# Another order of the attention sum, GpSimd's work and the odd batches' products in a kernel with pairwise Strassen K and V

## The reference

```python
def _L0_xattn_ref(x, context, context_mask, Wq, bq, Wkv, bkv, Wo, bo):
    q = x @ Wq + bq
    kv = context @ Wkv + bkv
    k, v = jnp.split(kv, 2, axis=-1)
    ...
    q = _larope(q, Lq)
    k = _larope(k, Lk)
    scores = jnp.einsum('bhqd,bhkd->bhqk', q, k) * SCALE
    scores = jnp.where(context_mask[:, None, None, :], scores, -jnp.inf)
    attn = jax.nn.softmax(scores, axis=-1)
    out = jnp.einsum('bhqk,bhkd->bhqd', attn, v)
    out = out.transpose(0, 2, 1, 3).reshape(B, Lq, H * hd)
    return out @ Wo + bo
...
x = x + _L0_xattn_ref(_layernorm(x, axis=-1), ctx_1024, mask_BxS2_bf1, ...)
x = x + _L0_attn_ref(_layernorm(x, axis=-1), ...)
x = x + _L0_ffn_ref(_layernorm(x, axis=-1), ...)
```

## Time and profile before

| what | value |
|---|---|
| median of 3 runs | 830.67 us (829.15 to 832.28) |
| profiled execution, its own time | 831.04 us |
| its span, first to last instruction | 829.2 us |
| cross attention, end of the last batch's step | about 585 us |
| TensorE busy | 760.4 us, 92% |
| VectorE busy | 574.8 us, 69% |
| ScalarE busy | 408.2 us, 49% |
| GpSimd busy | 340.0 us, 41% |
| mean granted TensorE clock | 0.961 |

### The profile page before, as it was taken

How to read it: one execution, slowest core, us unless ns; L and a number is a source line. 1 busy time by engine, 2 the same in 40 slices (tenths; PEclk the granted TensorE clock), 3 DMA queues, 4 the chain that set the end, 5 groups by cost and what they waited for, 6 DMA issues and landing times. The chain is left out here.

```text
span 829.2 us, 23209 instructions
## 1 busy us (share of the span) xinstructions
PE 760.4 (92%) x9494; PEld 660.5 (80%) x9495; DVE 574.8 (69%) x1293; ACT 408.2 (49%) x930; POOL 340.0 (41%) x364
## 2 busy tenths in 40 slices
PE   8999979979997997999899799798889999789997
PEld 7998869878896986888798688787667777668884
DVE  6766876975876686597577668746679998932236
ACT  5435646553563554555455464535447666213330
POOL 1654445454443644436354354522123222036740
PEclk9999999998999998999899999999999999969999
DMA  8211201111011010110101011013483234834548
GB/s 289 112 53 40 73 5 49 60 64 53 16 47 52 9 53 1 54 59 2 53 8 54 19 35 60 2 52 120 145 349 154 115 140 174 319 123 165 189 140 304
DMA packets 23317, 78.99 MB, mean 95 GB/s; under 512 B 3344, under 2 KB 4752, under 8 KB 20144
## 3 DMA queue, kind: packets, MB, share of 16 engines
q1 hardware_dynamic: 19536, 65.50, 21.7%
q0 software_dynamic: 3680, 12.06, 4.3%
HBM read 58.93 MB, written 18.61 MB: 94 GB/s over the span
## 5 line engine op out<-in xcount | busy, mean ns | idle before, releaser
L167 PE MATMUL quad<-wparts,othi 128*128 128x512 f32 (+1 forms) x104 | 49.2, 473 | 33.1 <-DVE otlo L1019 33.1
L501 POOL TENSOR_TENSOR wraw<-craw 128x516 f32<-128x516 f32 x14 | 18.6, 1326 | 135.9 <-issue 131.0
L1356 PE MATMUL bank<-ctx_parts_hi,wparts 128*128 128x258 f32 x224 | 68.7, 307 | 0.8 <-DVE ctx_parts_lo L890 0.7
L890 DVE TENSOR_TENSOR ctx_parts_lo<-craw,ctx_parts_hi 128x1032 fp32r<-128x1032 f32 (+1 forms) x56 | 64.8, 1158 | 2.6 <-ACT ctx_parts_hi L626 2.6
L1381 PE MATMUL bank<-wparts,ctx_parts_hi 128*128 128x256 f32 x224 | 64.6, 288 | 0.3 <-DVE kb_even L962 0.3
L1357 PE MATMUL bank<-ctx_parts_hi,wparts 128*128 128x258 f32 x224 | 63.5, 283 | 0.0
L1358 PE MATMUL bank<-ctx_parts_lo,wparts 128*128 128x258 f32 x224 | 63.4, 283 | 0.0
L1383 PE MATMUL bank<-wparts,ctx_parts_hi 128*128 128x256 f32 x224 | 63.0, 281 | 0.0
L1384 PE MATMUL bank<-wparts,ctx_parts_lo 128*128 128x256 f32 x224 | 62.8, 280 | 0.0
L626 ACT ACTIVATE ctx_parts_hi<-craw 128x1032 fp32r<-128x1032 f32 (+1 forms) x56 | 47.2, 843 | 26.9 <-POOL craw L509 26.6
L661 ACT ACTIVATE wraw<-wraw,nmax 128x257 f32<-128x257 f32 x96 | 47.9, 501 | 23.9 <-DVE nmax L983 23.9
(11 more groups left out here) (413 smaller groups left out, 2719.4 us busy)
## 6 DMA issues: line engine op xcount, KB each, us to landing
craw<-ctx_t_dram SPq DMA_DIRECT2D x32, 516.0 KB, 4.3
expert_lo<-weights_dram SPq DMA_DIRECT2D x8, 1024.0 KB, 12.2
expert_hi_scratch<-wraw SPq DMA_DIRECT2D x16, 512.0 KB, 2.6
wparts<-expert_hi_scratch SPq DMA_DIRECT2D x8, 1024.0 KB, 8.6
wraw<-weights_dram SPq DMA_DIRECT2D x6, 1024.0 KB, 4.9
expert_lo<-ffn_out_scratch SPq DMA_DIRECT2D x16, 256.0 KB, 5.2
x<-x_dram SPq DMA_DIRECT2D x8, 256.0 KB, 4.5
craw<-weights_dram SPq DMA_DIRECT2D x2, 1024.0 KB, 4.9
```

Source lines behind the costliest of these rows:

```text
L167: pe.matmul(psum, ahi(c), bhi(c), start=(c == 0), stop=False)
L890: dve.tensor_tensor(dst[1], src, dst[0].bitcast(F32), ALU.subtract).then_inc(s_clo, 1)
L1356: pe.matmul(psum, whi_i[:, i, cols], hi[:, i, :], start=own and i == 0, stop=False, skip_group_check=not own)
```

## The change

No instruction is added, removed or altered in size; only the order on four engines changes, from batch 3 to batch 30.

- **VectorE:** `o_sum(b-1)` comes first in every step, in front of `masked`; in even steps `v_sum(p, S_11)` too. `o_lo(b-1)` comes right behind `masked` in even steps (before: behind `k_cos` and the layer norm's statistics), and right behind `pair_parts` in odd steps.
- **GpSimd:** `o_bias(b-1)` comes first in every step. In odd steps `diagonals` and the first `k_sin` come ahead of `ctx_sums_early`. In even steps `ctx_sums_late` comes ahead of `diagonals`.
- **ScalarE:** `o_hi(b-1)` comes ahead of the exponentials in even steps, and ahead of `k_copy(p, 0, 4)` in odd ones. `k_copy(q, 0, 1)` comes ahead of `part_hi(q, O_T4)`. `v_copy(p, 5)` moves from the even step's start to the odd step's end.
- **TensorE, odd steps:** K product (0, 4) ahead of the transposes, (1, 1) ahead of (1, 3), (1, 6) ahead of the extra step, `diagonals_spread` and `attend` in the middle of the step, V product 2 behind 5 and behind K product (1, 4). Even steps keep their order.

```diff
--- before.py
+++ after.py
@@ -306,10 +306,10 @@
             L_HI, L_LO, L_PRODUCT, L_COPY, L_SUM = range(1, 6)
 
 
-            K_PRODUCTS = ((0, 2), (0, 5), (0, 1), (0, 6), (0, 3), (0, 7), (1, 2), (1, 5), (0, 4), (1, 3), (1, 1), (1, 6),
+            K_PRODUCTS = ((0, 2), (0, 5), (0, 1), (0, 6), (0, 3), (0, 7), (1, 2), (1, 5), (0, 4), (1, 1), (1, 3), (1, 6),
                           (1, 7), (1, 4))
             K_COPIES = ((0, 5), (0, 1), (0, 6), (1, 5), (0, 4), (1, 1), (1, 6), (1, 4))
-            V_PRODUCTS = (2, 5, 1, 6, 3, 7, 4)
+            V_PRODUCTS = (5, 2, 1, 6, 3, 7, 4)
             V_COPIES = (5, 1, 6, 4)
 
             def k_product_of(q, c, k):
@@ -570,24 +570,24 @@
                         if b == PLAIN - 2:
                             ctx_sums_late(q)
                     elif b % 2 == 1:
+                        o_bias(b - 1)
+                        diagonals(b)
+                        if b < B - 1:
+                            k_sin(b + 1, 0)
                         if q <= PAIR_LAST:
                             ctx_sums_early(q)
-                        o_bias(b - 1)
-                        if b < B - 1:
-                            k_sin(b + 1, 0)
-                        diagonals(b)
                         if b < B - 1:
                             k_sin(b + 1, 1)
                         ln_and_bias(t, j)
                         if b < B - 1:
                             k_sin(b + 1, 2)
                     else:
+                        o_bias(b - 1)
                         for i in range(3):
                             k_sin(b + 1, i)
-                        o_bias(b - 1)
-                        diagonals(b)
                         if q <= PAIR_LAST:
                             ctx_sums_late(q)
+                        diagonals(b)
                         ln_and_bias(t, j)
                 ln_pool(pool, TILES + 1)
                 o_bias(B - 1)
@@ -790,10 +790,10 @@
                     p, q = b // 2, b // 2 + 1
                     more = q <= PAIR_LAST
                     last = t == TILES - 1
-                    v_copy(p, 5)
                     v_copy(p, 1)
                     if more:
                         part_hi(q, O_X1)
+                    before_o_hi(b)
                     exp(b, 0)
                     exp(b, 1)
                     v_copy(p, 6)
@@ -805,12 +805,11 @@
                     for g in range(G):
                         pt_evac(b, g)
                     v_copy(p, 4)
-                    before_o_hi(b)
                     if more:
                         part_hi(q, O_T32)
                         k_copy(q, 0, 5)
+                        k_copy(q, 0, 1)
                         part_hi(q, O_T4)
-                        k_copy(q, 0, 1)
                     if j == 0:
                         ln_apply(t + 1, x[:, 0 if last else t + 1, :])
                     if more:
@@ -824,23 +823,24 @@
                     for g in range(G):
                         exp(b, g)
                     k_copy(p, 1, 5)
+                    before_o_hi(b)
+                    k_copy(p, 0, 4)
                     pt_evac(b, 0)
                     pt_evac(b, 1)
-                    k_copy(p, 0, 4)
+                    k_copy(p, 1, 1)
                     pt_evac(b, 2)
                     pt_evac(b, 3)
-                    k_copy(p, 1, 1)
-                    next_mask(b)
-                    before_o_hi(b)
+                    k_copy(p, 1, 6)
                     if j == 1:
                         xt_hi(t + 1)
-                    k_copy(p, 1, 6)
                     if j == 3:
                         qt_evac(t + 1)
+                    next_mask(b)
                     if q <= PAIR_LAST:
                         part_hi(q, O_T1)
+                    v_copy(p, 5)
                     k_copy(p, 1, 4)
-                    if b == PLAIN - 1:
+                    if b == PAIR_FIRST * 2 - 1:
                         w_hi(WO)
                     if last:
                         act.wait_ge(s_qmm, TILES)
@@ -1136,13 +1136,14 @@
                     p, q = b // 2, b // 2 + 1
                     more = q <= PAIR_LAST
                     last = t == TILES - 1
+                    o_sum(b - 1)
+                    v_sum(p, S_11)
                     begin_step(b, j)
-                    v_sum(p, S_11)
+                    o_lo(b - 1, (b - 1) % BT)
                     if more:
                         part_lo(q, O_X1)
                     v_sum(p, S_12)
                     v_sum(p, S_22)
-                    o_sum(b - 1)
                     inverse_sums(b)
                     pair_parts(b)
                     if more:
@@ -1153,7 +1154,6 @@
                         if t == 2:
                             dve.wait_ge(s_x, 16 * (TILES - 1))
                         ln_stats(t + 1, x[:, 0 if last else t + 1, :])
-                    o_lo(b - 1, (b - 1) % BT)
                     if more:
                         part_lo(q, O_T32)
                     if j == 0:
@@ -1171,21 +1171,21 @@
                 def odd_step(b, t, j):
                     p, q = (b + 1) // 2, (b + 3) // 2
                     last = t == TILES - 1
+                    o_sum(b - 1)
                     begin_step(b, j)
                     k_sum(p, 0, S_12)
                     k_sum(p, 0, S_22)
                     if j == 3:
                         q_rotate(t + 1)
-                    o_sum(b - 1)
                     inverse_sums(b)
                     pair_parts(b)
+                    o_lo(b - 1, (b - 1) % BT)
                     k_cos(b + 1, 0)
                     k_sum(p, 1, S_11)
                     k_cos(b + 1, 1)
-                    o_lo(b - 1, (b - 1) % BT)
+                    k_sum(p, 1, S_12)
                     if j == 1:
                         xt_lo(t + 1)
-                    k_sum(p, 1, S_12)
                     k_sum(p, 1, S_22)
                     if q <= PAIR_LAST:
                         part_lo(q, O_T1)
@@ -1561,18 +1561,18 @@
                     k_product(p, 0, 7)
                     k_product(p, 1, 2)
                     k_product(p, 1, 5)
+                    k_product(p, 0, 4)
                     probs_transposed(b)
-                    k_product(p, 0, 4)
+                    k_product(p, 1, 1)
                     k_product(p, 1, 3)
-                    k_product(p, 1, 1)
+                    k_product(p, 1, 6)
                     extra_step(b, t, j)
-                    k_product(p, 1, 6)
-                    v_product(p, 2)
+                    diagonals_spread(b)
+                    attend(b, j)
                     k_product(p, 1, 7)
                     v_product(p, 5)
                     k_product(p, 1, 4)
-                    diagonals_spread(b)
-                    attend(b, j)
+                    v_product(p, 2)
                     v_product(p, 1)
 
                 def last_step(b, j):
```

## The result

| | before | after |
|---|---|---|
| median | 830.71 us (829.15 to 832.28, 4 runs) | 777.09 us (776.16 to 778.46, 4 runs) |
| profiled execution | 831.04 us | 776.16 us |
| mean granted TensorE clock | 0.961 | 0.986 |

The ratio of the times is 0.9356, with a 95% interval from 0.9331 to 0.9381: 6.4% faster, 53.6 us. The prediction said 43.7 us. The time lies 0.1 us inside its range (777 to 804) and outside the 781 to 794 that it took for likeliest.

A forecast was written before the change was run, and what follows sets the result against it. The prediction took TensorE's own work to bound the kernel, held up by waits for `o_lo`. It put 55.8 us removed against 12.1 added, 43.7 net, giving 787.0 us, 5.3% faster, likeliest 781 to 794, range 777 to 804.

The forecast's parts named there:

- The bound and the main wait: TensorE's work sets the end; seven output products wait for VectorE's `o_lo`, late only by its place: 33.1 us saved.
- The slow clock, 13.9: TensorE's seven output products run at a clock that fell during the wait before them; full clock saves 13.9 us.
- K product (0, 6), 3.9: Last K product of even steps waits 0.64 us for `k_copy(q, 0, 1)` behind a `part_hi`; turning them round saves 3.9.
- Odd steps, 4.9 saved and 1.4 added: `o_bias` first frees `o_hi` and K copies, 4.9 us saved; K products sharing one bank, delayed by copies, add 1.4.
- undisturbed ones take 16.04: Odd steps that nothing delays take 16.04 us; the 13 together exceed 13 times that by 4.9 us.
- Diagonals with j = 2, 6.0: GpSimd's second diagonal, behind VectorE's `part_lo(O_T32)`, ends at 14.0, 1.0 us after TensorE comes; six steps add 6.0.
- O_T32 with j = 0, 1.4: `part_lo(O_T32)` ends about when K product (0, 6) needs it; 0.2 us latency in seven steps adds 1.4, below 0.
- Batches 4 and 30, 3.3: `o_sum` and a `v_sum` ahead of VectorE's masks delay V product 7 by about 1.65 us; both batches add 3.3.
- The first: Rival: diagonals, O_T32 and copies come just in time, only batches 4 and 30 cost; 778.5 us, chance 0.12.
- VectorE did not become the bound: Rival: VectorE becomes the bound, masks come 1.5 us late in 13 odd steps, 16 us more; 803 us, chance 0.15.
- The third: Rival: slower, as TensorE waits at `diagonals_spread` in all 13 even steps and the clock falls; 846 us at w = 3, chance 0.04.
- The fourth: Rival: `o_hi` sits behind `part_hi(O_X1)` on ScalarE, so the stall only moves; about 827 us, chance 0.04.

The follow-up runs named there:

- experiment 1: Changed kernel with `o_lo` of the even steps back behind `k_cos` and the statistics on VectorE; 804.16 us, ratio 0.9706 to the kernel before.
- experiment 4: Kernel before with 16 added matmuls, their result overwritten, in front of each of the seven output products that wait; 817.11 us, ratio 0.9851.
- experiment 5: Kernel before with four moves in even steps alone: `o_sum` first, `o_lo` behind the masks, `o_bias` first, `o_hi` ahead of the exponentials; 784.64 us, ratio 0.9453.
- experiment 6: Kernel before with one move: in odd steps GpSimd's `o_bias` ahead of the early context sums; 827.79 us, ratio 0.9977.
- experiment 3: Changed kernel with GpSimd's diagonals ahead of the late sums again in even steps; 777.36 us, ratio 0.9366 to the kernel before.
- experiment 7: Changed kernel with diagonals ahead of the late sums at j = 2 only, and the first `v_sum` behind the masks in batches 4 and 30; 774.39 us, ratio 0.9332.
- second execution of after: The changed kernel itself run once more, unaltered, for comparison on the same chip; 777.31 us, ratio 0.9368 to the kernel before.
- experiment 2: Changed kernel with the odd steps' TensorE products, their ScalarE copies, `v_copy(p, 5)` and `next_mask` in the old order; 780.30 us, ratio 0.9411.

## Why the prediction came out as it did

**The number: inside the range by luck.** The median is 777.09 and the bound was 777; the four times go from 776.16 to 778.46. The terms taken away were sized nearly right. Those added came to 5.2 us where the prediction had 12.1, and that is most of the 8.6 by which the steps gained more than forecast.

**The bound and the main wait: right.** TensorE's own work sets the end, and `o_lo` was late by its place. With it moved back, 19.9 us of waiting return (experiment 1). `o_lo` ended 3.5 us after the scores where the prediction had 3.7. The size was 1.2 too small: in the kernel before the output product's first matmul starts 5.0 us behind the matmul ahead of it (5.17 in batch 4), after the change 0.12. That is 34.3 us for seven, where the idle time in the matmul rows says 33.1 and that in the weight loads' rows 34.6:

```profile
PEld quad L167 <- DVE otlo L1019: 34.6, 7, 5.1
```

The matmul row counts from the end of the matmul ahead, but without a wait the next one would start before that end.

**The slow clock, 13.9: right.** 33.54 us for seven stretches became 19.52, so 14.0, and experiment 4 took 13.3 of it away without moving `o_lo`.

**K product (0, 6), 3.9: right in size, wrong in cause.** The steps with j = 2 without the diagonals' wait take 90.1 us against 94.04 before, 3.9 less. The prediction put the wait down to `k_copy(q, 0, 1)` standing behind a `part_hi`; experiment 5 keeps that order and gains 4.2. The product also waited for `part_lo(O_T32)`, which ended only 0.1 before the copy. Both came 1 us earlier once `o_sum` no longer stood in front of `k_cos`. That reading is from the traces; `o_sum` alone was not moved.

**Odd steps, 4.9 saved and 1.4 added: both sizes off.** The mechanism of the 4.9 is confirmed by experiment 6, with 3.5 in the profiled execution and 2.5 between the medians. But the step "undisturbed ones take 16.04" failed: that length held 0.37 us of waiting in every second step, in the rows of the weight loads, which I hadn't read. And of the bank chain, put at 1.4, nothing was seen: after has no such wait. The prediction had 13 x 16.04 and about 1.4, 209.9; it was 208.06, 1.9 less, though 2.6 of it are pauses that the prediction did not have (last section): the steps without one take 15.60 and 16.04.

**Diagonals with j = 2, 6.0: mechanism right, size twice too large.** The steps lost 2.8 (0.47 each, experiments 3 and 7), of which the odd steps behind them give back 1.5, and none appeared with j = 0, as forecast. The step that failed is the start: it had the late sums end at 11.2 and the first diagonal near 12.2 because of shared time. Measured from the scores they ended at 11.1 and 11.8, and the second, blocked by `part_lo`, at 13.4 in place of 14.0. That 0.6 is most of the difference. The 0.47 per step is all in the starts of TensorE's rows: in batch 14 the first matmul of `attend` starts 0.90 behind the last K matmul (269.68 to 270.58), before the change 0.44 (292.84 to 293.28). The row of the weight load shows 0.39 of it, that of the matmul 0.18. Here the rule of the Trainium skill (SBUF — State Buffer, "Who interferes with whom"), by which the second of two such instructions fully blocks, fits the rows better than mere slowing. The trace agrees: the diagonal takes 1.60 us behind a `part_lo` and 0.66 when first, and mere slowing was put at 1.07. For the time it decided little: the prediction had 14.0 and 6.0 us by blocking, 13.3 and 1.8 by slowing (from its own 13.08 that is 1.3), and 13.4 and 2.8 were measured, nearer the second. The order of blocking was right and its start was not: `part_lo` began at 11.3, ahead of the first diagonal's end, and not behind it.

**O_T32 with j = 0, 1.4: not there.** The steps took 14.97. The lower bound of 0 was the right end. That the margin is thin is shown by experiment 3, where the wait appeared in all seven of these steps with the late sums one diagonal pair later.

**Batches 4 and 30, 3.3: right in kind.** Batch 4 took 1.34 more than its like (16.31 against 14.97), batch 30 1.08 more than before, together 2.4. Only some 0.5 of that is due to the `v_sum` ahead of the masks (experiment 7: 0.20 and 0.28). In experiment 5, where it is behind the masks, batch 30 takes 13.75 too, so the rest comes with the early attention sum; by the order of the rows that is `o_sum` ahead of the masks, which was not tried alone.

**What is left.** Against the 43.7 forecast the steps gave 52.25: 3.2 from the diagonals, 1.4 from O_T32, 1.9 from the odd steps, 0.9 from batches 4 and 30, less 0.3 in batch 3. 1.5 us more came from the steps with j = 0, which saved 48.5 without batch 4's cost where the prediction's wait and clock make 47.1. The starts of TensorE's rows account for it: 1.2 are the wait's true length (34.3), and 0.3 lie behind the stretches, where the slow clock lasted on in batch 20. It is no gain from the late sums' new place, for behind the output product these steps took 2.65 us before, batch 20 apart, and take 2.65 now. What that place does is keep a wait away: with diagonals first and `o_lo` early they take 15.33 (experiment 3) and 15.29 (experiment 5), with the sums first 14.97. The prediction had costed the diagonals' move at a loss only, and did not ask what it spares the sums' readers.

**The rivals.** The first, everything covered at 778.5, gave the nearest time, but by the wrong path: the diagonals were not covered, and other terms made up for it. VectorE did not become the bound: the odd steps got shorter, and from batch 4 to 30 no row of after, matmul or weight load, waits for VectorE; the one wait for a sum, 0.4 us, is in batch 3. The third didn't come, since the wait at `diagonals_spread` was 0.2 at most in these steps (0.4 by the weight loads). The fourth neither: the wait did not move elsewhere.

## What to carry to other kernels

An instruction with all its inputs ready that another engine will need goes where its inputs are ready; here half of the 53 us hung on the place of one instruction. A wait of the bounding engine is to be priced with what it does to the clock, and its small waits are to be looked for in the weight loads too, where those of 0.37 us stood that no matmul row showed. What a wait costs is the distance between the starts of two matmuls, with and without it; the idle time in a matmul's row was 0.2 to 0.3 us too small here. Where the work of two engines collides, putting one instruction ahead of another moves a cost between kinds of steps: look at each kind by itself and at the step behind it, for the best order may differ between them.

## What was not expected of the hardware

**One and the same wait, two clocks.** In experiment 1 seven waits of 2.85 to 2.9 us, with the same work ahead and behind, were followed four times by the lower clock (stretches of 4.12 to 4.43 us at 0.61 to 0.67) and three times by the full one (2.89 to 2.91 at 1.00). The seven waits of the kernel before, 33.1 us in all, brought it down each time; the one of 1.94 us and those of 1.1 us in experiment 4 did not. All ten profiled executions have a wait for weights at the start of self attention, 3.24 to 3.35 us long (before at 586.88, after at 533.26), and the lower clock followed it each time.

**Pauses without a releaser.** What makes the longest odd steps of after is no wait for another engine. TensorE within the scores of batch 15:

```profile
273.83 0.37 PE L1398 MATMUL bank<-ksin,qt 32*32 32x257 f32 x1 [0.21 <-issue]
```

The row shows 0.21 us of idle time that the profile puts down to nothing ("issue"), that of the weight load 0.69, and this step takes 16.84 us where its like takes 16.05; batch 27 takes 17.11 with idle times of 0.52 and 1.01. In the second execution of after batch 15 took 16.66 and batch 27 16.02, in experiment 2 16.62 and 17.37; in experiments 3 and 7 neither shows any. So it is worth 0.6 to 1.3 us where it falls, in part at the same place, and depends on the kernel. The traces of all runs have nine weight loads in the scores, from batch 4 on, with such an idle time of over 0.4 us. Ahead of each of the nine, by 2.2 to 3.0 us, a transfer of 16 KB began that the trace calls "instruction". But of the steps of batches 4 to 30 in all runs 58 others have such a transfer between 1.6 and 0.5 us ahead of their scores, as those nine have, and no such pause. So this is a lead and no cause shown; no run here was made for it.
